# Two graph layers with residual normalisation: the rounding and splitting of x for group g+2 stands late in step g instead of at the begin of step g+1

## The chip, the cores and the metric

The kernel runs on one core of one Trainium2 chip. The metric is the device time in microseconds of one execution; lower is better.

## The reference

x has 128 graphs of 64 nodes with 512 features, in float32; adj is one 64 x 64 adjacency matrix with ones on its diagonal.

```python
x = layernorm(x + einsum('bnf,nm->bmf', x, adj * adj) + bias)        # layer 0, gives h
z_l, z_g, v = h @ W_lang.T, h @ W_grav.T, h @ W_V.T                  # layer 1
A_l = max(zn @ zn.T, 0) * not_eye             # zn: rows of z_l over their norms
A_g = exp(-|z_g[n] - z_g[m]|**2 / (2 sigma**2)) * not_eye
K = w_l * row_stochastic(A_l * adj) + (1 - w_l) * row_stochastic(A_g * adj)
out = layernorm(h + (K @ v) @ W_O.T)
```

## The kernel before

Two graphs fill the 128 partitions and make one pair p; four pairs make a group (NP = 4), and there are 16 groups (NG = 16). Every float32 matmul is made of three matmuls on rounded halves: each operand is split into a part _hi (rounded, by ScalarE) and a part _lo (the remainder, by VectorE, or by GpSimd for x), and hi·hi, hi·lo and lo·hi are added up in PSUM.

The weights are folded at the start, so that a group needs these pieces of work:

- x of a group comes in by one DMA into x_sb. ScalarE rounds it into x_hi (`split_x`, two instructions of 1024 columns), GpSimd subtracts into x_lo (`split_x`, four instructions of 512 columns).
- Layer 0: TensorE (`layer0`), VectorE adds the bias and takes statistics (`add_y`, `count_y`), GpSimd turns them into scales (`scale_y`), ScalarE normalises (`normalise_h`).
- h is transposed on TensorE (`transpose_h`) and split into hT_hi (ScalarE, `hi_hT`) and hT_lo (VectorE, `lo_hT`, L769).
- Twelve projections (`project` 0 to 11, L357) through a ring of three PSUM banks; each is split by `hi_proj` (ScalarE, L562) and `lo_proj` (VectorE, L774). Projection k may begin when `lo_proj` of the projection three before it is done.
- The Gram matrices of two pairs at a time (`gram` 0 and 1, L377) are copied out by ScalarE (`copy_p`); VectorE takes their diagonals (`diagonals`: four L784 instructions, then two L792) and GpSimd makes column factors of them (`columns`).
- Similarities, one group behind: TensorE transposes (`transpose_p`, L390 and L397), VectorE adds and weighs (`add_p` L805, `weigh` L812 and L816), forms sums and coefficients (`coefficients`, from L826 on) and K (`combine`, L843); TensorE transposes K (`transpose_k`, L408), it is split again (`hi_kt`, `lo_kt`), and `apply_k` (L421) multiplies.
- The result gets the residual, statistics, scales (`add_z`, `count_z`, `scale_z`) and `normalise_out`, and four DMAs store it.

A step g of the loop does the projections and Gram matrices of group g, layer 0 and the transposes of group g+1, and the similarities, K and the output of group g-1. The order on each engine is written out by hand and kept by semaphores alone; nothing reorders it. On TensorE a step runs: project 0, transpose_p(g-1, 0), project 1 to 3, transpose_p(g-1, 1), project 4, transpose_k(g-1, 0), project 5 and 6, apply_k 0 and 1, project 7, transpose_k(g-1, 1), layer 0 of pairs 0 and 1, project 8, apply_k 2 and 3, layer 0 of pairs 2 and 3, project 9 and 10, gram 0, transpose_h 0 and 1, project 11, transpose_h 2 and 3, gram 1. The last group has an order of its own, with no work for a group after it, and so no split of x; up to its project 6 the order on TensorE and up to transpose_k 0 that on VectorE is the one of a step.

Waits that matter here:

```python
# TensorE
project:     if k == 0: wait hT_split >= NP*g + NP        # all four lo_hT (L342)
             wait proj_split >= NPROJ*g + k - NRING + 1   # lo_proj three before (L347)
transpose_k: wait k_done; wait s2_done >= 2*g + 2         # add_p of both halves (L401, L404)
# VectorE
diagonals:   wait p_copied;   lo_hT: wait hT_hi_done;   lo_proj: wait proj_hi
# GpSimd
split_x:     wait x_hi_done >= 2*g + p//2 - 1
# the DMA queue of SyncE
load(g):     wait x_lo_done >= NP*g
```

Of the kernel before, what the change touches and what calls it, by code (L numbers as in the profile page):

```python
# [18 lines left out]
def bass_two_layer_graph_resnorm(  # L19
# [19 lines left out]
    NP = 4  # L39
    NG = B * N // (R * NP)  # L40
# [15 lines left out]
    def ring_of(k):  # L56

        return (NSETUP + k) % NRING
# [5 lines left out]
    with ctx:  # L64
# [182 lines left out]
        def out_rows(g):  # L247

            return x_sb if isinstance(g, int) and g == NG - 1 else o_sb
# [9 lines left out]
        def settle(engine):  # L259

            engine.nop(nofuse=True)
# [290 lines left out]
        def proj_dst(k, which):  # L552

            kind, j = PROJ[k]
            if kind == "u":
                return (u_hi, u_lo)[which][:, j, :]
            return (yT_hi, yT_lo)[which][:, j, kind, :]

        @block.scalar
        def _(act):  # L560
            def copy(dst, src, scale=1.0):
                return act.activation(dst, src, ACT.Copy, scale=scale)  # L562

            def split_x(g, c):
                if c == 0:
                    act.wait_ge(x_loaded, 16 * g)

                    act.wait_ge(l0_done, NP * g)
                s = slice(2 * c, 2 * c + 2)
                copy(x_hi[:, s, :], x_sb[:, s, :]).then_inc(x_hi_done, 1)  # L570
# [16 lines left out]
            def hi_proj(g, k):  # L587
                act.wait_ge(proj_done, NPROJ * g + k + 1)
                copy(proj_dst(k, 0), ring[ring_of(k)][:, :]).then_inc(proj_hi, 1)
# [8 lines left out]
            def exp_g(g, q):  # L598
                act.wait_ge(s2_done, 2 * g + q + 1)
                act.activation(E_g[:, :, :], S2[:, :, G, :], ACT.Exp, scale=inv_2s2[:, 0:1]).then_inc(exp_done, 1)  # L600

            def scale_l(g, q):
                act.wait_ge(coef_done, 2 * g + q + 1)
                for pp in range(2):
                    last = act.activation(K_l[:, pp, :], X_l[:, pp, :], ACT.Copy, scale=coef[:, pp:pp + 1])
                last.then_inc(kl_done, 1)
# [5 lines left out]
            def normalise_out(g, p):  # L612
                act.wait_ge(z_scale, 2 * g + p // 2 + 1)
                act.activation(out_rows(g)[:, p, :], out_rows(g)[:, p, :], ACT.Identity, scale=z_rs[:, p:p + 1],  # L614
                               bias=z_nb[:, p:p + 1]).then_inc(o_ready, 1)

            def step(g, par, tail=True):
                split_x(g + 1, 0)
                split_x(g + 1, 1)
                hi_proj(g, 0)  # L620
                hi_proj(g, 1)
                if tail:
                    exp_g(g - 1, 0)
                hi_proj(g, 2)
                if tail:
                    scale_l(g - 1, 0)
                hi_proj(g, 3)
                if tail:
                    exp_g(g - 1, 1)
                hi_proj(g, 4)  # L630
                if tail:
                    hi_kt(g - 1, 0)
                    scale_l(g - 1, 1)
                hi_proj(g, 5)
                hi_proj(g, 6)
                hi_proj(g, 7)
                if tail:
                    hi_kt(g - 1, 1)
                    normalise_out(g - 1, 0)
                    normalise_out(g - 1, 1)  # L640
                hi_proj(g, 8)
                normalise_h(g + 1, 1 - par, 0)
                normalise_h(g + 1, 1 - par, 1)
                if tail:
                    normalise_out(g - 1, 2)
                hi_proj(g, 9)
                if tail:
                    normalise_out(g - 1, 3)
                hi_proj(g, 10)
                copy_p(g, 0)  # L650
                normalise_h(g + 1, 1 - par, 2)
                normalise_h(g + 1, 1 - par, 3)
                hi_hT(g + 1, 1 - par, 0)
                hi_hT(g + 1, 1 - par, 1)
                hi_proj(g, 11)
                hi_hT(g + 1, 1 - par, 2)
                hi_hT(g + 1, 1 - par, 3)
                copy_p(g, 1)
# [43 lines left out]
                hi_hT(0, 0, p)  # L702
            hi_value(M_hi, 3 * DC)

            step(0, 0, tail=False)
            step(1, 1)
            with act.Fori(2, NG - 2, 2) as g:
                step(g, 0)
                step(g + 1, 1)
            step(NG - 2, 0)  # L710
            g = NG - 1
            hi_proj(g, 0)
            hi_proj(g, 1)
# [356 lines left out]
        @block.gpsimd  # L1070
        def _(pool):
            def split_x(g, p):
                pool.wait_ge(x_hi_done, 2 * g + p // 2 - 1)
                pool.tensor_tensor(x_lo[:, p, :], x_sb[:, p, :], x_hi[:, p, :], ALU.subtract).then_inc(x_lo_done, 1)  # L1074

            def scale_of(stats, ve_done, rs_done, scale, mv, ve, nm, rs, nb, d, q):

                pq = slice(2 * q, 2 * q + 2)
                pool.wait_ge(stats, d + 1)
                settle(pool)  # L1080
                pool.tensor_scalar(ve[:, pq], mv[:, pq, 1], LN_EPS, None, ALU.add).then_inc(ve_done, 1)  # L1081
                pool.wait_ge(ve_done, d + 1)
                pool.tensor_tensor(rs[:, pq], ve[:, pq], pow_neg_half[:, :], ALU.pow).then_inc(rs_done, 1)
                pool.tensor_scalar(nm[:, pq], mv[:, pq, 0], -1.0, None, ALU.mult).then_inc(rs_done, 1)
                pool.wait_ge(rs_done, 2 * d + 2)
                pool.tensor_tensor(nb[:, pq], nm[:, pq], rs[:, pq], ALU.mult).then_inc(scale, 1)  # L1086

            def scale_y(g, q):
                scale_of(y_stats, y_ve_done, y_rs_done, y_scale, y_mv, y_ve, y_nm, y_rs, y_nb, 2 * g + q, q)

            def scale_z(g, q):
                scale_of(z_stats, z_ve_done, z_rs_done, z_scale, z_mv, z_ve, z_nm, z_rs, z_nb, 2 * g + q, q)

            def columns(g, q):
                d = 2 * g + q
                pool.wait_ge(sq_done, d + 1)
                settle(pool)

                pool.tensor_scalar(sq_floor[q][:, :], sq[q][:, L, :], EPS * EPS, None, ALU.max).then_inc(floor_done, 1)
                pool.wait_ge(floor_done, d + 1)  # L1100
                pool.tensor_tensor(inv_norm[q][:, :], sq_floor[q][:, :], pow_neg_half[:, :],
                                   ALU.pow).then_inc(cols_ready, 1)

                pool.tensor_scalar(sq_eps[q][:, :], sq_floor[q][:, :], 2 * EPS, None, ALU.mult).then_inc(sq_eps_done, 1)
                pool.wait_ge(cols_ready, d + 1)
                pool.wait_ge(sq_eps_done, d + 1)
                pool.tensor_tensor(floors[q][:, 0:2], sq_eps[q][:, :], inv_norm[q][:, :],
                                   ALU.mult).then_inc(floors_ready, 1)

            def step(g, tail=True):  # L1110
                if tail:
                    columns(g - 1, 1)
                for p in range(NP):
                    split_x(g + 1, p)
                for q in range(2):
                    if tail:
                        scale_z(g - 1, q)
                    scale_y(g + 1, q)
                columns(g, 0)

            pool.memset(adj_bd[:, :], 0.0).then_inc(adj_zeroed, 1)
            pool.memset(ident[:, :], 0.0).then_inc(ident_ready, 1)
            pool.wait_ge(ident_ready, 1)
            pool.affine_select(out=ident[:, :], in_=ident[:, :], compare_op=ALU.not_equal, fill=1.0, base=0,
                               pattern=[[-1, R]], channel_multiplier=1).then_inc(ident_ready, 1)
            pool.memset(pow_neg_half[:, :], -0.5)
            pool.memset(floors[0][:, 2:4], EPS)
            pool.memset(floors[1][:, 2:4], EPS).then_inc(pow_ready, 1)
            pool.wait_ge(pow_ready, 1)
            for q in range(2):  # L1130
                scale_y(0, q)

            step(0, tail=False)
            step(1)
            with pool.Fori(2, NG - 2, 1) as g:
                step(g)
            step(NG - 2)
            g = NG - 1
            columns(g - 1, 1)
            scale_z(g - 1, 0)  # L1140
            columns(g, 0)
            columns(g, 1)
            scale_z(g - 1, 1)
            for q in range(2):

                pool.wait_ge(o_ready, NP * (g - 1) + 2 * q + 2)
                scale_z(g, q)
# [27 lines left out]
```

## Time and profile before

| | |
|---|---|
| device time, median of 3 runs | 702.46 us (702.32 to 703.02) |
| profiled execution | span 701.2 us from the first to the last instruction; no other time of it is given |
| TensorE busy | 671.6 us, 96% of the span |
| VectorE busy | 536.3 us, 76% |
| ScalarE busy | 345.4 us, 49% |
| GpSimd busy | 211.0 us, 30% |
| granted TensorE clock | 0.997 of full speed (mean) |
| one step in the middle, from project 0 to project 0 | 41.00 us |

Busy time is the time in which an engine had an instruction under way. Matmuls overlap, so that each has some 390 ns while the next one starts 230 ns after it. Of an instruction that is held up inside the engine, the time held up counts as its duration.

### The profile page before, as it was taken

Reading aid. Unit: us, or ns where it says so; the run is one execution under the profiler, and the core shown is the slowest. Engines: PE = TensorE matmul, PEld = TensorE weight load, DVE = VectorE, ACT = ScalarE, POOL = GpSimd, SP = SyncE. Lnnn points to the kernel's source line nnn. Section 1 sums busy time; section 2 is a strip of 40 time slices with the busy share of each in tenths; the row PEclk is TensorE's granted clock in tenths of the full one; section 3 lists DMA queues with packets and bytes.
Section 4 is the critical chain, followed back from the end, with each engine's and each line's share of the span. In section 5 each row is a group of like instructions: output and inputs, shape, how many; then the busy total and the mean of one; then the engine's idle time right before and its main releaser. Section 6 shows DMA issues by size and latency. Waiting matters only on the chain. (4 is left out here: it accounts for less than half of the span.)

```text
span 701.2 us, 11745 instructions
## 1 busy us (share of the span) xinstructions
PE 671.6 (96%) x3579; PEld 570.4 (81%) x3579; DVE 536.3 (76%) x1523; ACT 345.4 (49%) x614; POOL 211.0 (30%) x454
## 2 busy tenths in 40 slices
PE   8999999999999999999999999999999999999994
PEld 7888878787887878788787878878787887878883
DVE  6835795977879597786959778695977969697786
ACT  5633546355354535445453544545454454545433
POOL 0121413333341333334133333413333341233022
PEclk9999999999999999999999999999999999999998
DMA  7210020111102011110201111020111102001002
GB/s 286 91 38 24 5 86 31 61 60 61 61 3 87 30 60 60 60 60 0 90 30 60 60 60 60 0 90 30 60 60 60 55 5 90 31 0 61 0 31 91
DMA packets 20406, 38.33 MB, mean 55 GB/s; under 512 B 1824, under 2 KB 1824, under 8 KB 20384
## 3 DMA queue, kind: packets, MB, share of 16 engines
q1 hardware_dynamic: 20384, 38.05, 15.0%
q8 instruction: 12, 0.20, 0.1%
q14 instruction: 10, 0.08, 0.0%
HBM read 21.27 MB, written 16.78 MB: 54 GB/s over the span
## 5 line engine op out<-in xcount | busy, mean ns | idle before, releaser
L357 PE MATMUL ring<-hT_hi,T_hi 128*128 128x512 f32 x320 | 129.5, 405 | 0.0
L357 PE MATMUL ring<-hT_hi,T_lo 128*128 128x512 f32 x320 | 125.2, 391 | 0.0
L357 PE MATMUL ring<-hT_lo,T_hi 128*128 128x512 f32 x320 | 125.0, 391 | 0.0
L562 ACT ACTIVATE yT_hi<-ring 128x512 fp32r<-128x512 f32 x128 | 75.7, 591 | 71.0 <-PE ring L357 70.4
L774 DVE TENSOR_TENSOR yT_lo<-ring,yT_hi 128x512 fp32r<-128x512 f32 x128 | 86.1, 682 | 26.7 <-ACT yT_hi L562 26.7
L357 PE MATMUL ring<-M_hi,hT_hi 128*128 128x512 f32 x256 | 101.5, 397 | 0.0
L357 PE MATMUL ring<-M_hi,hT_lo 128*128 128x512 f32 x256 | 100.2, 391 | 0.0
L357 PE MATMUL ring<-M_lo,hT_hi 128*128 128x512 f32 x256 | 99.8, 390 | 0.0
L1074 POOL TENSOR_TENSOR x_lo<-x_sb,x_hi 128x512 fp32r<-128x512 f32 x60 | 77.0, 1315 | 18.5 <-ACT x_hi L562 18.5
L614 ACT ACTIVATE o_sb<-o_sb,z_nb,z_rs 128x512 f32<-128x512 f32 x60 | 47.1, 809 | 63.9 <-POOL z_nb L1086 63.9
L784 DVE CUSTOM_DVE_ANT_0 diag_scr<-P_sb,ident 128x128 f32<-128x128 f32 x128 | 29.7, 288 | 62.9 <-ACT P_sb L562 62.9
L1081 POOL TENSOR_SCALAR z_ve<-z_mv 128x2 f32<-128x2 f32 x32 | 7.0, 219 | 217.2 <-DVE z_mv L870 212.5
L377 PE MATMUL bank_p<-yT_hi,hT_hi 128*128 128x256 f32 x248 | 71.4, 288 | 0.1
L357 PEld LDWEIGHTS ring<-hT_hi,T_lo 128*128 128x128 f32 x320 | 60.1, 188 | 13.4
L357 PEld LDWEIGHTS ring<-hT_hi,T_hi 128*128 128x128 f32 x320 | 60.2, 188 | 12.7 <-DVE yT_lo L774 1.3
L377 PE MATMUL bank_p<-yT_hi,hT_lo 128*128 128x256 f32 x248 | 70.1, 283 | 0.0
L377 PE MATMUL bank_p<-yT_lo,hT_hi 128*128 128x256 f32 x248 | 70.1, 283 | 0.0
L357 PEld LDWEIGHTS ring<-hT_lo,T_hi 128*128 128x128 f32 x320 | 60.3, 188 | 10.6
L774 DVE TENSOR_TENSOR u_lo<-ring,u_hi 128x512 fp32r<-128x512 f32 x64 | 44.3, 692 | 26.7 <-ACT u_hi L562 26.5
L579 ACT ACTIVATE h_sb<-h_sb,y_nb,y_rs 128x512 f32<-128x512 f32 x64 | 48.7, 808 | 25.3 <-POOL y_nb L1086 25.3
L357 PEld LDWEIGHTS ring<-M_hi,hT_lo 128*128 128x128 f32 x256 | 48.0, 188 | 10.4
L357 PEld LDWEIGHTS ring<-M_lo,hT_hi 128*128 128x128 f32 x256 | 48.2, 188 | 9.9
(159 smaller groups left out, 1421.9 us busy)
## 6 DMA issues: line engine op xcount, KB each, us to landing
x_sb<-in_x_dram SPq DMA_DIRECT2D x15, 1024.0 KB, 5.2
out_dram<-o_sb SPq DMA_DIRECT2D x60, 256.0 KB, 2.0
x_sb<-in_x_dram SPq DMA_DIRECT2D x2, 512.0 KB, 5.2
w_raw<-in_L_gnn_W_lang_dram SPq DMA_DIRECT2D x1, 1024.0 KB, 6.2
o_sb<-in_L_gnn_W_grav_dram SPq DMA_DIRECT2D x1, 1024.0 KB, 8.6
h_sb<-in_L_gnn_W_V_dram SPq DMA_DIRECT2D x1, 1024.0 KB, 10.7
w_raw<-in_L_gnn_W_O_dram SPq DMA_DIRECT2D x1, 1024.0 KB, 7.8
out_dram<-x_sb SPq DMA_DIRECT2D x4, 256.0 KB, 2.0
```

The costliest lines, as they stand in the source:

```text
L357: last = pe.matmul(bank[:, :], a, b, start=n == 0, stop=n == len(terms) - 1)
L377: last = pe.matmul(p_bank(g, q)[:, pp, :, :], a, b, start=n == 0, stop=n == len(terms) - 1)
L562: return act.activation(dst, src, ACT.Copy, scale=scale)
L579: act.activation(h_sb[par][:, p, :], h_sb[par][:, p, :], ACT.Identity, scale=y_rs[:, p:p + 1], bias=y_nb[:, p:p + 1]).then_inc(h_ready, 1)
L614: act.activation(out_rows(g)[:, p, :], out_rows(g)[:, p, :], ACT.Identity, scale=z_rs[:, p:p + 1], bias=z_nb[:, p:p + 1]).then_inc(o_ready, 1)
L774: dve.tensor_tensor(proj_dst(k, 1), ring[ring_of(k)][:, :], proj_dst(k, 0), ALU.subtract).then_inc(proj_split, 1)
L784: last = dve.tensor_tensor_reduce(out=diag_scr[:, 2 * pp + s, :], in0=P_sb[q][:, pp, s, :], in1=ident[:, :], scale=1.0, scalar=0.0, op0=AL ...
L1074: pool.tensor_tensor(x_lo[:, p, :], x_sb[:, p, :], x_hi[:, p, :], ALU.subtract).then_inc(x_lo_done, 1)
L1081: pool.tensor_scalar(ve[:, pq], mv[:, pq, 1], LN_EPS, None, ALU.add).then_inc(ve_done, 1)
```

## The change

`split_x` of ScalarE for the next group stood at the head of a step, ahead of `hi_proj(g, 0)`. Now step g holds the one for group g+2, behind `normalise_out(g-1, 3)` and ahead of `hi_proj(g, 10)`. On GpSimd the four instructions stood behind `columns(g-1, 1)`; now they stand behind `scale_y(g+1, 1)` and ahead of `columns(g, 0)`. Group 1 is split ahead of step 0, and step 14 splits nothing. The waits in `split_x` are the same: x has landed, layer 0 of the group before is done (it frees x_hi and x_lo), and for GpSimd x_hi is there. The load of the next x waits for x_lo as before.

```diff
@@ ScalarE
-            def step(g, par, tail=True):
-                split_x(g + 1, 0)
-                split_x(g + 1, 1)
+            def step(g, par, tail=True, ahead=True):
                 hi_proj(g, 0)
                 hi_proj(g, 1)
...
                 hi_proj(g, 9)
                 if tail:
                     normalise_out(g - 1, 3)
+                if ahead:
+                    split_x(g + 2, 0)
+                    split_x(g + 2, 1)
                 hi_proj(g, 10)
                 copy_p(g, 0)
...
+            split_x(1, 0)
+            split_x(1, 1)
             step(0, 0, tail=False)
...
-            step(NG - 2, 0)
+            step(NG - 2, 0, ahead=False)
@@ GpSimd
-            def step(g, tail=True):
+            def step(g, tail=True, ahead=True):
                 if tail:
                     columns(g - 1, 1)
-                for p in range(NP):
-                    split_x(g + 1, p)
                 for q in range(2):
                     if tail:
                         scale_z(g - 1, q)
                     scale_y(g + 1, q)
+                if ahead:
+                    for p in range(NP):
+                        split_x(g + 2, p)
                 columns(g, 0)
...
+            for p in range(NP):
+                split_x(1, p)
             step(0, tail=False)
...
-            step(NG - 2)
+            step(NG - 2, ahead=False)
```

## Rows read from the trace of the kernel before

**Rows 1.** The page: busy time, share of the span and instructions of each engine
```profile
PE 671.6 (96%) x3579; PEld 570.4 (81%) x3579; DVE 536.3 (76%) x1523; ACT 345.4 (49%) x614; POOL 211.0 (30%) x454
```

**Rows 2.** Waits of TensorE: what waited for what, us in total, times, longest
```profile
PE bank_pt L408 <- DVE S L805: 17.1, 14, 1.2
```

**Rows 3.** Timeline of TensorE in two steps: start us, us, instruction, [idle before <-releaser]
```profile
290.13 0.38 PE L397 MATMUL bank_r<-ident,inv_norm 128*128 128x128 f32 x2
290.48 0.50 PE L357 MATMUL ring<-hT_hi,T_hi 128*128 128x512 f32 x1
...
331.25 0.38 PE L397 MATMUL bank_r<-ident,inv_norm 128*128 128x128 f32 x2
331.47 0.50 PE L357 MATMUL ring<-hT_hi,T_hi 128*128 128x512 f32 x1
...
334.10 0.39 PE L357 MATMUL ring<-hT_hi,T_lo 128*128 128x512 f32 x1
335.73 0.41 PE L408 MATMUL bank_pt<-ident,K_sb 128*128 128x128 f32 x2 [1.24 <-DVE S L805]
```

**Rows 4.** Timeline of VectorE in that step, up to that wait
```profile
328.72 0.78 DVE L816 CUSTOM_DVE_ANT_0 X_l<-X,mask 128x128 f32<-128x128 f32 x1
...
329.44 1.37 DVE L816 CUSTOM_DVE_ANT_0 X_l<-X,mask 128x128 f32<-128x128 f32 x1
...
330.74 0.68 DVE L774 TENSOR_TENSOR yT_lo<-ring,yT_hi 128x512 fp32r<-128x512 f32 x1
331.34 0.76 DVE L826 SCALAR_TENSOR_TENSOR X_g<-E_g,mask 128x128 f32<-128x128 f32 x1
...
334.90 0.68 DVE L805 TENSOR_TENSOR S<-bank_pt,P_sb 128x512 f32<-128x512 f32 x1
```

**Rows 5.** Timeline of GpSimd around that step's begin
```profile
313.74 0.20 POOL L1086 TENSOR_TENSOR y_nb<-y_nm,y_rs 128x2 f32<-128x2 f32 x1
...
326.81 5.14 POOL L1074 TENSOR_TENSOR x_lo<-x_sb,x_hi 128x512 fp32r<-128x512 f32 x4
```

**Rows 6.** Timeline of VectorE in the last group, the same stretch
```profile
657.13 0.29 DVE L816 CUSTOM_DVE_ANT_0 X_l<-X,mask 128x128 f32<-128x128 f32 x1
...
661.25 0.68 DVE L805 TENSOR_TENSOR S<-bank_pt,P_sb 128x512 f32<-128x512 f32 x1
```

**Rows 7.** Timeline of TensorE in the last group, the same stretch
```profile
659.66 0.38 PE L397 MATMUL bank_r<-ident,inv_norm 128*128 128x128 f32 x2
659.79 0.47 PE L357 MATMUL ring<-hT_hi,T_hi 128*128 128x512 f32 x1
...
662.40 0.39 PE L357 MATMUL ring<-hT_hi,T_lo 128*128 128x512 f32 x1
662.63 0.38 PE L408 MATMUL bank_pt<-ident,K_sb 128*128 128x128 f32 x2
```

**Rows 8.** Timeline of ScalarE, late in a step and at the next begin
```profile
312.36 0.81 ACT L614 ACTIVATE o_sb<-o_sb,z_nb,z_rs 128x512 f32<-128x512 f32 x1
...
316.19 0.60 ACT L562 ACTIVATE P_sb<-bank_p 128x512 f32<-128x512 f32 x1 [2.35 <-PE bank_p L377]
...
323.98 2.00 ACT L562 ACTIVATE x_hi<-x_sb 128x1024 fp32r<-128x1024 f32 x2
```

**Rows 9.** Timeline of VectorE, late in the step: diagonals to lo_hT
```profile
316.82 0.29 DVE L784 CUSTOM_DVE_ANT_0 diag_scr<-P_sb,ident 128x128 f32<-128x128 f32 x1 [2.26 <-ACT P_sb L562]
...
317.86 0.48 DVE L792 TENSOR_SCALAR P_sb<-P_sb,sq 128x128 f32<-128x128 f32 x2
318.71 0.69 DVE L769 TENSOR_TENSOR hT_lo<-bank_x,hT_hi 128x512 fp32r<-128x512 f32 x1 [0.37 <-ACT hT_hi L562]
...
321.57 0.68 DVE L769 TENSOR_TENSOR hT_lo<-bank_r,hT_hi 128x512 fp32r<-128x512 f32 x1
```

**Rows 10.** Timeline of TensorE, the begin of the next step's project 0
```profile
323.28 0.40 PE L357 MATMUL ring<-hT_hi,T_hi 128*128 128x512 f32 x1
```

**Rows 11.** GpSimd's subtractions, all: xcount, ns min/median/max, first and last start us
```profile
L1074 POOL TENSOR_TENSOR x_lo<-x_sb,x_hi x60: 1280/1301/1354, 43.9 to 618.0; 128x512 fp32r<-128x512 f32 x60
```

## The prediction, made before the result was known

> **What bounds the kernel now.** I began with the page. TensorE is busy for 671.6 of 701.2 us and no other engine passes 76% [rows 1], so a change pays only where TensorE stands still, or costs where it makes it stand still. The next view is TensorE's waits. One line carries nearly all of it: transpose_k (L408) waits for VectorE's add_p (L805), 14 times, 17.1 us in all, never over 1.2 us [rows 2]. Fourteen times is once in each of steps 1 to 14. The timeline of one step shows its true size: the matmul before it starts at 334.10, transpose_k at 335.73 [rows 3], 1.63 us apart, where the same two stand 0.23 us apart when nothing is late [rows 7]. So the stall is 1.40 us (the view of waits counts from the modelled end of the matmul, some 0.16 us later: 17.1 / 14 = 1.22, and 1.22 + 0.16 = 1.38). Over 14 steps I take 14 x 1.38 = 19.3 us.
>
> A second, small one stands just ahead: project 4 after transpose_p(g-1, 1) starts 0.22 us after L397 in one step and 0.35 us in its neighbour [rows 3], where 0.13 us is undisturbed [rows 7]. Project 4 waits for lo_proj 1, which is the L774 from 330.74 to 331.42 [rows 4], 0.05 us before 331.47. That is 0.09 and 0.22 us in turn, 7 x 0.31 = 2.2 us; call it 2.0, since step 14 has the small value.
>
> Why is VectorE late? Its timeline has two L816 of 0.78 and 1.37 us and one L826 of 0.76 us [rows 4]. In the last group the same L816 takes 0.29 us [rows 6]. GpSimd tells the rest: its four subtractions for x_lo run from 326.81 to 331.95, without a gap, 1.3 us each [rows 5, 11], so they end near 328.1, 329.4, 330.7 and 331.95. The slow instructions end at 329.50, 330.81 and 332.10: each some 0.15 us behind the end of one GpSimd instruction. VectorE is held until the GpSimd instruction under way is over, and gets in one such instruction between two of GpSimd's. The L774 in the middle, which has one input in PSUM, keeps its 0.68 us [rows 4]. L816 and L826 have both inputs in SBUF. Lost: (0.78 - 0.29) + (1.37 - 0.29) + (0.76 - 0.29) = 2.04 us in each step.
>
> The last group is the experiment that the kernel makes by itself: it has no x_lo beside it. There add_p ends at 661.93 [rows 6], 0.70 us before transpose_k wants to start, and both stalls are gone [rows 7].
>
> **What the change removes.** The x_lo work leaves the stretch of L816 and L826. VectorE gets its 2.04 us back, more than the 1.40 us that TensorE waits, and the last group shows the margin that is left, 0.70 us. Both stalls vanish in the 14 steps: 19.3 + 2.0 = 21.3 us. The two ScalarE roundings, 2.00 us from 323.98 [rows 8], also leave the step's begin. That is worth nothing: they lay in ScalarE's idle time before project 0 was done, and VectorE's lo_proj 0 then waits for TensorE anyhow, in the last group too, where they are missing.
>
> **What it adds: the new place.** On ScalarE normalise_out(g-1, 3) ends at 313.17 [rows 8]. Two roundings follow, 313.1 to 315.1, then hi_proj 10 of some 0.6 us (the length of the copy at 316.19) to 315.7. copy_p waits for gram 0 until 316.19 [rows 8], so it isn't moved, and nothing behind it is. Their cover is the 2.35 us for which ScalarE idled ahead of that copy; without it, they would push hi_hT and the lo_hT behind it.
>
> GpSimd is free from 313.94 [rows 5]. It starts when the first rounding of 1.0 us is done, at about 314.19, and needs 5.14 us as before [rows 5]: pieces end near 315.5, 316.8, 318.05 and 319.33. Beside them VectorE does `diagonals`: four L784 from 316.82 [rows 9]. L784 is the same custom operation as L816, with both inputs (P_sb, ident) in SBUF, so I let it be held the same way. In the trace before no L784 has an x_lo beside it. Bounds: each at 0.29 us as now (no hold), or held to the end of the last GpSimd piece. I take the second, by the row of L816. The third piece is under way at 316.82: the first L784 ends at 318.2, the second at 319.33 + 0.15 = 319.48, the others 0.21 us apart at 319.69 and 319.91, instead of 317.75 (0.11 us ahead of L792 at 317.86 [rows 9]). So VectorE is 2.16 us late there.
>
> By the Trainium skill ("SBUF — State Buffer", Who interferes with whom) a VectorE instruction with two SBUF inputs contends with a GpSimd instruction that reads SBUF, and the second to issue blocks fully. By that rule L784 collides in its new company as L816 did in the old; it gives the same sum as the row of L816, and speaks against getting the full 21.3 us. No row of L784 shows it yet.
>
> What is behind L784 on VectorE: two L792, then lo_hT 0 and 1, lo_proj 11, lo_hT 2 and 3. The L792 start 0.11 us after the last L784, and the next could follow 0.40 us later. The five run at 0.60 us intervals, and the last takes 0.68. So the last lo_hT ends 0.51 + 4 x 0.60 + 0.68 = 3.59 us after the last L784: 323.50. Today it ends at 322.25, since it holds two pauses of 0.37 us for ScalarE (the one before 318.71 is in [rows 9], the other stands before lo_proj 11). Project 0 of the next step waits for it and starts at 323.28 now [rows 10]. With some 0.1 us from VectorE's end to TensorE's start (0.15 between L805 and L408 [rows 3, 4]) it starts at 323.60: a new stall of 0.3 us. In steps 1 to 14 that is 14 x 0.3 = 4.2 us.
>
> Who else waits: `columns(g, 0)` on GpSimd moves behind x_lo and the late diagonals, from 317.9 to about 320.0. Its four small instructions take under 2 us, and its reader, transpose_p, stands behind project 0, which begins at 323.3 and lasts 2.8 us. SyncE's load for the next x is released by x_lo near 319.4 instead of 331.95, after the four stores of that step, and its data is wanted some 35 us later. It costs nothing, and a transfer of 5 us could be late by 30 before it did. Ahead of step 0 the split of group 1 is what step 0 did first, at the same place.
>
> **The sum.** Span 701.2 - 21.3 + 4.2 = 684.1 us. The span misses 1.26 us of the median (702.46); I keep this: 685.4 us.
>
> **The rivals.**
>
> *A. As above*, both stalls gone, a new one of 0.1 to 0.7 us before project 0: 682.6 to 691.0, likeliest 685.4.
>
> *B. The new place is free*: L784 isn't held, or fewer pieces hit it. VectorE has 1.03 us between 322.25 and 323.28, and 0.74 us of pauses; a delay under 1.7 us doesn't show. Then 702.46 - 21.3 = 681.2 us. For it: my value of 2.16 us is only 0.4 us past this. Against it: 316.82 falls right behind the begin of the third piece.
>
> *C. The stall moves and eats the gain*, one mechanism: x_lo starts later than 314.2, since the roundings stand behind two normalise_out, which hang on a chain of statistics through VectorE and GpSimd. Each us later is one us more of stall, as the diagonals can't end before the last piece. At x_lo from 315.4 on the new stall is 1.5 us and the change is worth nothing: 702.5 us. In between, at 0.8 to 1.4 us, 692.4 to 700.8.
>
> *D. Slower*: VectorE holds GpSimd up as well. If three of the four pieces each waited for one VectorE instruction of 0.7 us, x_lo would end 2.1 us later, the new stall would be 2.4 us, and the time 702.46 - 21.3 + 14 x 2.4 = 714.8 us. It decides from 1.2 us of such delay on. Against it: 60 pieces lie between 1280 and 1354 ns, with VectorE busy beside most of them [rows 11].
>
> *E. VectorE's gain is not what frees transpose_k*: then only the new stall counts, 702.46 + 4.2 = 706.7. The last group speaks against it.
>
> **How the numbers follow.** A 0.66, B 0.19, C's gains 0.07 and its point of no gain 0.02, D 0.04, E 0.02. The predicted time is that of A. For the range I take B whole (681.2, less 0.5 for phase) and A up to its bound of a 0.7 us stall: 680.7 to 691.0; what is left out, C, D and E, is 0.15. Of no change I call what lies within 0.2%, 1.4 us, about what a measurement of this kernel can tell. Faster: A, B and C's gains, 0.92. Same 0.03. Slower 0.05.
>
> **What the profile after would show.** Right: L816 at 0.29 us everywhere and no wait of L408 on L805; L784 with maxima near 1.3 us in `diagonals(g, 0)`, and the L784 of `diagonals(g, 1)` at 0.29; a new wait of TensorE at project 0 (L357) on hT_lo (L769), some 0.3 us, 14 times; a step of about 39.8 us instead of 41.0; x_lo starting 9.1 us before the last gram's end. Wrong: L784 at 0.29 throughout (B), x_lo starting less than 8.2 us before the last gram's end, or pieces of x_lo over 1.6 us (C, D), or L408 still waiting (E).

## The result and the profile after

| | median | runs | |
|---|---|---|---|
| before | 702.54 us | 4 | 702.32 to 703.02 |
| changed | 685.2 us | 4 | 684.88 to 685.32 |

The ratio is 0.975, with a 95% interval of 0.9739 to 0.9761: 17.3 us faster, where 17.1 were forecast (702.46 - 685.4). The profiled execution took 685.29 us with a span of 683.5 us. In the changed kernel the lines of VectorE and GpSimd stand three or more further down: `diagonals` is L787 (was L784), `weigh` L819 (L816), `coefficients` L829 (L826), `lo_hT` L772 (L769), x_lo L1077 (L1074).

TensorE's share on the page, to be read beside [rows 1]:

```profile
PE 669.0 (98%) x3579; PEld 571.0 (84%) x3579; DVE 532.2 (78%) x1523; ACT 345.6 (51%) x614; POOL 210.4 (31%) x454
```

The waits of TensorE. The row of transpose_k in [rows 2] is gone, and in the loop one wait long enough for this view is left, at project 0 (L357). The other rows belong to the setup ahead of the loop, or, at L421, to the last group:

```profile
PE ring L475 <- DVE yT_lo L947: 1.9, 1, 1.9
PE bank_r L483 <- POOL ident L1128: 1.7, 1, 1.7
PE bank_r L421 <- issue: 0.8, 1, 0.8
PE ring L357 <- DVE hT_lo L772: 0.5, 1, 0.5
...
```

The timeline of TensorE at the two places of [rows 3], now back to 0.14 and 0.23 us:

```profile
324.32 0.38 PE L397 MATMUL bank_r<-ident,inv_norm 128*128 128x128 f32 x2
324.46 0.47 PE L357 MATMUL ring<-hT_hi,T_hi 128*128 128x512 f32 x1
...
327.06 0.39 PE L357 MATMUL ring<-hT_hi,T_lo 128*128 128x512 f32 x1
327.29 0.38 PE L408 MATMUL bank_pt<-ident,K_sb 128*128 128x128 f32 x2
```

The durations of `weigh` and `diagonals` over the whole run (count, then ns min/median/max). `weigh` (L819) has lost its long ones, `diagonals` (L787) has them now:

```profile
L819 DVE CUSTOM_DVE_ANT_0 X_l<-X,mask x64: 284/291/295, 82.7 to 665.1; 128x128 f32<-128x128 f32 x64
...
L787 DVE CUSTOM_DVE_ANT_0 diag_scr<-P_sb,ident x128: 280/289/1375, 70.8 to 660.2; 128x128 f32<-128x128 f32 x128
```

The late place itself, first GpSimd, then VectorE beside it, to be read against [rows 9]:

```profile
306.86 5.10 POOL L1077 TENSOR_TENSOR x_lo<-x_sb,x_hi 128x512 fp32r<-128x512 f32 x4 [0.25 <-ACT x_hi L562]
312.70 0.30 POOL L1102 TENSOR_SCALAR sq_floor<-sq 128x2 f32<-128x2 f32 x1 [0.74 <-DVE sq L787]
```

```profile
309.61 1.20 DVE L787 CUSTOM_DVE_ANT_0 diag_scr<-P_sb,ident 128x128 f32<-128x128 f32 x1 [0.68 <-ACT P_sb L562]
...
310.74 1.37 DVE L787 CUSTOM_DVE_ANT_0 diag_scr<-P_sb,ident 128x128 f32<-128x128 f32 x1
...
312.04 0.28 DVE L787 CUSTOM_DVE_ANT_0 diag_scr<-P_sb,ident 128x128 f32<-128x128 f32 x1
...
312.25 0.28 DVE L787 CUSTOM_DVE_ANT_0 diag_scr<-P_sb,ident 128x128 f32<-128x128 f32 x1
...
313.05 0.68 DVE L772 TENSOR_TENSOR hT_lo<-bank_x,hT_hi 128x512 fp32r<-128x512 f32 x1
...
315.44 0.68 DVE L772 TENSOR_TENSOR hT_lo<-bank_r,hT_hi 128x512 fp32r<-128x512 f32 x1
```

The last of four GpSimd pieces ends at 311.96. Two of the four L787 are held, 1.20 and 1.37 us, and the second ends at 312.11, 0.15 us behind the piece. The diagonals take 2.92 us instead of 0.93. The last lo_hT ends at 316.12, and TensorE's project 0 starts 0.13 us later, at 316.25:

```profile
315.96 0.28 PE L377 MATMUL bank_p<-yT_hi,hT_lo 128*128 128x256 f32 x1
316.25 0.49 PE L357 MATMUL ring<-hT_hi,T_hi 128*128 128x512 f32 x1
316.58 0.40 PE L357 MATMUL ring<-hT_lo,T_hi 128*128 128x512 f32 x1
```

0.29 us lie between 315.96 and 316.25, where matmuls of the gram stand 0.12 us apart: a stall of 0.17 us. A stall read in this way, from the distance of two starts, is called a stall by the starts below. The modelled end of the last gram matmul (0.28 us) swallows it, so the view of waits doesn't list it; it is found by the starts alone.

### The profile page after: what moved, and what is told of

Same layout as the page of the kernel before. It is cut to its first block, busy times and chain, and to the rows that moved or that the text cites. A ratio compares the mean times of both kernels' runs of the same rounds, so it can differ in the third digit from the quotient of the medians.

```text
span 683.5 us, 11745 instructions
## 1 busy us (share of the span) xinstructions
PE 669.0 (98%) x3579; PEld 571.0 (84%) x3579; DVE 532.2 (78%) x1523; ACT 345.6 (51%) x614; POOL 210.4 (31%) x454
## 4 chain that ended last, share of the span: by engine, by line
PE 92%; DVE 3%; ACT 2%; DMA 1%; issue 1%; POOL 1%; SPq 0%; POOLq 0%; DVEq 0%
PE ring L357 56%; PE bank_p L377 12%; PE ring L475 4%; PE bank_x L318 3%; PE bank_p L318 3%; PE bank_k L421 3%; PE bank_r L421 3%; PE bank_pt L390 2%; PE bank_r L397 1%; DMA w_raw<-in_L_gnn_W_lang_dram 1%; PE bank_pt L336 1%; PE bank_r L336 1%; PE bank_k L336 1%; PE bank_pt L408 1%; PE bank_x L336 1%
## 5 line engine op out<-in xcount | busy, mean ns | idle before, releaser
L357 PE MATMUL ring<-hT_hi,T_hi 128*128 128x512 f32 x320 | 130.5, 408 | 0.6 <-DVE hT_lo L772 0.5
L357 PE MATMUL ring<-hT_hi,T_lo 128*128 128x512 f32 x320 | 125.4, 392 | 0.0
L357 PE MATMUL ring<-hT_lo,T_hi 128*128 128x512 f32 x320 | 124.7, 390 | 0.0
L777 DVE TENSOR_TENSOR yT_lo<-ring,yT_hi 128x512 fp32r<-128x512 f32 x128 | 87.5, 684 | 35.3 <-ACT yT_hi L562 35.3
L357 PE MATMUL ring<-M_hi,hT_hi 128*128 128x512 f32 x256 | 101.5, 396 | 0.0
L357 PE MATMUL ring<-M_hi,hT_lo 128*128 128x512 f32 x256 | 100.2, 391 | 0.0
L357 PE MATMUL ring<-M_lo,hT_hi 128*128 128x512 f32 x256 | 99.9, 390 | 0.0
L1077 POOL TENSOR_TENSOR x_lo<-x_sb,x_hi 128x512 fp32r<-128x512 f32 x60 | 76.4, 1301 | 22.4 <-ACT x_hi L562 22.4
L787 DVE CUSTOM_DVE_ANT_0 diag_scr<-P_sb,ident 128x128 f32<-128x128 f32 x128 | 56.4, 495 | 28.0 <-ACT P_sb L562 28.0
L357 PEld LDWEIGHTS ring<-hT_hi,T_hi 128*128 128x128 f32 x320 | 60.1, 188 | 13.6 <-issue 3.0
L357 PEld LDWEIGHTS ring<-hT_hi,T_lo 128*128 128x128 f32 x320 | 60.1, 188 | 13.4
L357 PEld LDWEIGHTS ring<-hT_lo,T_hi 128*128 128x128 f32 x320 | 60.3, 188 | 10.8
L357 PEld LDWEIGHTS ring<-M_hi,hT_lo 128*128 128x128 f32 x256 | 48.0, 188 | 10.3
L357 PEld LDWEIGHTS ring<-M_lo,hT_hi 128*128 128x128 f32 x256 | 48.1, 188 | 9.9
```

Of the source, the lines that this page charges most:

```text
L357: last = pe.matmul(bank[:, :], a, b, start=n == 0, stop=n == len(terms) - 1)
L777: dve.tensor_tensor(proj_dst(k, 1), ring[ring_of(k)][:, :], proj_dst(k, 0), ALU.subtract).then_inc(proj_split, 1)
L787: last = dve.tensor_tensor_reduce(out=diag_scr[:, 2 * pp + s, :], in0=P_sb[q][:, pp, s, :], in1=ident[:, :], scale=1.0, scalar=0.0, op0=AL ...
```

## The experiments

The time agrees with the forecast, but an agreement of one sum proves none of its terms. The theory is that GpSimd's subtractions hold VectorE's instructions with two inputs in SBUF, at the old place and at the new. Its rivals: ScalarE's roundings ahead of hi_proj 0 were the cost; any work of GpSimd would hold VectorE; or the small remainder at project 0 has another cause. The first four kernels ran on one chip (before: 702.64 us there), the last four on one chip as well (before: 702.76 us). Code cuts leave lines out at "...", and the declarations of a scratch tile and of semaphores.

### The roundings alone moved

```diff
 # on the kernel before; GpSimd unchanged
@@ ScalarE, step(g)
-                split_x(g + 1, 0)
-                split_x(g + 1, 1)
                 hi_proj(g, 0)
...
                     normalise_out(g - 1, 3)
+                if ahead:
+                    split_x(g + 2, 0)
+                    split_x(g + 2, 1)
                 hi_proj(g, 10)
```

> The kernel before, with ScalarE's roundings of x (x_hi of g+2) in the new late place and GpSimd's four subtractions left at the begin of the step. Theory (the subtractions hold VectorE's L816 and L826): nothing is gained, 701.5 to 703.5 us, L816 keeps its 0.8 and 1.4 us and transpose_k still waits 1.4 us in 14 steps. Rival (ScalarE's 2.0 us ahead of hi_proj 0 were what made the step late): most of the gain comes from this alone, 684 to 690 us.

Measured: 702.73 us, ratio 0.9999 (0.9989 to 1.0008). No part of the gain comes from moving ScalarE's roundings alone. The wait of transpose_k is as before, and `weigh` is still held:

```profile
PE bank_pt L408 <- DVE S L808: 17.3, 14, 1.3
```

```profile
L819 DVE CUSTOM_DVE_ANT_0 X_l<-X,mask x64: 283/293/1373, 82.1 to 682.4; 128x128 f32<-128x128 f32 x64
```

It also shows that the roundings cost nothing at the late place.

### The subtractions made tiny, at the old place

```diff
 # on the kernel before
-    pool.tensor_tensor(x_lo[:, p, :], x_sb[:, p, :], x_hi[:, p, :], ALU.subtract)
+    pool.tensor_tensor(x_lo[:, p, 0:2], x_sb[:, p, 0:2], x_hi[:, p, 0:2], ALU.subtract)
```

> The kernel before, with GpSimd's four subtractions of the loop on 2 of 512 columns each (the rest of x_lo keeps what group 0 left there), everything at its old place, ScalarE's roundings at the begin of the step too. Theory: both waits of TensorE go, 702.5 - 21.3 = 681.2 us. Rival (ScalarE's roundings at the begin cost something as well): over 684 us, with a wait left in the first projections.

Measured: 680.7 us (680.6 to 680.87), ratio 0.9683 (0.9666 to 0.9699). This is the price of the subtractions at the old place: 702.64 - 680.7 = 21.9 us, against 21.3 forecast. No wait of transpose_k is left, with ScalarE's roundings at the step's begin, and no L816 is held:

```profile
L816 DVE CUSTOM_DVE_ANT_0 X_l<-X,mask x64: 284/291/295, 82.2 to 660.6; 128x128 f32<-128x128 f32 x64
```

### GpSimd busy, but only writing

```diff
 # on the kernel before, in split_x of GpSimd; x_lo becomes zero
-    pool.tensor_tensor(x_lo[:, p, :], x_sb[:, p, :], x_hi[:, p, :], ALU.subtract).then_inc(x_lo_done, 1)
+    settle(pool)
+    pool.memset(scratch[:, :], 0.0).then_inc(scratch_done, 1)      # 1024 columns
+    pool.wait_ge(scratch_done, NP * (g - 1) + p + 1)
+    settle(pool)
+    pool.memset(x_lo[:, p, :].bitcast(fp32), 0.0).then_inc(x_lo_done, 1)
```

> The kernel before, with each subtraction replaced by two GpSimd memsets (1024 columns of a scratch tile, then the 512 of x_lo, which is thus zero), so GpSimd is busy at the old place and writes SBUF but reads nothing there. Theory that VectorE's second SBUF input shares a read path with GpSimd: L816 and L826 at 0.29 us although memsets run beside them, no wait of transpose_k, 681 to 683 us. Rival (any GpSimd instruction beside holds VectorE, or memory traffic as such): L816 ends each time just behind the end of a memset, and transpose_k waits again, in so far as the memsets reach to 328.7 and beyond in the step.

Measured: 680.69 us, ratio 0.9683 (0.9662 to 0.9703), the time of the kernel with tiny subtractions. GpSimd was busy over the same stretch, some 1.5 us for each pair. Its timeline in one step, and VectorE's beside it:

```profile
160.63 0.96 POOL L1077 MEMSET scratch<- 128x1024 f32 x1
161.70 0.53 POOL L1080 MEMSET x_lo<- 128x512 f32 x1
162.17 0.95 POOL L1077 MEMSET scratch<- 128x1024 f32 x1
```

```profile
161.01 0.29 DVE L818 CUSTOM_DVE_ANT_0 X_l<-X,mask 128x128 f32<-128x128 f32 x1
...
162.04 0.28 DVE L828 SCALAR_TENSOR_TENSOR X_g<-E_g,mask 128x128 f32<-128x128 f32 x1
...
162.25 0.29 DVE L828 SCALAR_TENSOR_TENSOR X_g<-E_g,mask 128x128 f32<-128x128 f32 x1
```

L818 lies wholly inside the memset from 160.63 to 161.59 and takes its 0.29 us; the L828 at 162.25 lies inside the one from 162.17. Over the whole run none of them is held, and transpose_k doesn't wait:

```profile
L818 DVE CUSTOM_DVE_ANT_0 X_l<-X,mask x64: 283/290/294, 82.0 to 660.4; 128x128 f32<-128x128 f32 x64
...
L828 DVE SCALAR_TENSOR_TENSOR X_g<-E_g,mask x64: 280/286/291, 83.1 to 661.9; 128x128 f32<-128x128 f32 x64
```

So it is not GpSimd's activity as such, nor its writing, that holds VectorE. What differs is that a memset reads nothing from SBUF. It is also another operation in pieces of other lengths; no run here tells the reading from these. The result fits the sentence of the Trainium skill ("SBUF — State Buffer", Who interferes with whom) that a VectorE instruction with two SBUF inputs contends with a GpSimd instruction that reads SBUF and not with one that only writes it; here 1.37 us beside the subtraction and 0.29 beside the memset.

### One piece more at the late place

```diff
 # on the changed kernel, GpSimd, ahead of the four subtractions
+                    pool.wait_ge(x_hi_done, 2 * g + 3)
+                    pool.tensor_tensor(x_lo[:, 0, :], x_sb[:, 0, :], x_hi[:, 0, :], ALU.subtract).then_inc(extra_done, 1)
+                    pool.wait_ge(extra_done, g + 1)
                     for p in range(NP):
                         split_x(g + 2, p)
```

> The changed kernel with one more subtraction of 512 columns (the one of pair 0 done twice) ahead of the four in the late place, so that the last piece ends 1.3 to 1.4 us later. Theory (project 0 waits for lo_hT, which waits for the diagonals, which wait for the last piece): the wait of 0.2 us becomes 1.5 to 1.6, and the time 685.2 + 14 x 1.35 = 704 us, the whole gain gone. Rival (there is slack behind the diagonals, and the 0.2 us at project 0 has another cause): under 690 us.

Measured: 701.4 us (701.22 to 701.72), ratio 0.998 (0.997 to 0.9989). One more subtraction of 1.3 us on an engine that is 31% busy costs 16 us, nearly the whole gain. TensorE's wait is where the theory puts it:

```profile
PE ring L358 <- DVE hT_lo L773: 17.1, 13, 1.4
```

It is in 13 steps, not 14, which is half of the difference to the 704 us expected. The other half: against the 685.29 us of the changed kernel measured again (below), each costs 16.1 / 13 = 1.24 us on average instead of 1.35. In step 0 there is no output of a group before, so ScalarE and GpSimd get to the split earlier: the first subtraction starts 11.1 us ahead of project 0 of step 1.

### The changed kernel again, and its subtractions made tiny

> The changed kernel once more, on the chip of the three below: 685.2 us, ratio 0.975, project 0 late by 0.17 us in most steps.

Measured: 685.29 us (684.96 to 685.41), ratio 0.9752 (0.9738 to 0.9765). Its trace has the same 13 stalls at project 0, eleven of them of 0.15 to 0.19 us.

```diff
 # on the changed kernel
-    pool.tensor_tensor(x_lo[:, p, :], x_sb[:, p, :], x_hi[:, p, :], ALU.subtract)
+    pool.tensor_tensor(x_lo[:, p, 0:2], x_sb[:, p, 0:2], x_hi[:, p, 0:2], ALU.subtract)
```

> The changed kernel with the four subtractions of the loop on 2 of 512 columns each (the rest of x_lo keeps what group 0 left there). It prices all that x_lo still costs in the late place. Theory: the wait at project 0 (2.7 us in sum over the steps in the trace) goes, 682.5 us. Rival (the late place costs more than that wait, for example through ScalarE's late hi_proj 10): no gain over 685.2, or a wait left elsewhere.

Measured: 680.77 us (680.6 to 680.94). It is the same time as with tiny subtractions at the old place (680.7), so ScalarE's roundings and the earlier load of x cost nothing in either place. The subtractions cost 685.29 - 680.77 = 4.5 us at the new place. I had expected 2.7, the sum of the stalls by the starts. What I left out is that TensorE starts up less densely after a wait: the first matmul at 316.25 is followed after 0.33 us, and without the wait, in this kernel, after 0.24:

```profile
313.76 0.40 PE L357 MATMUL ring<-hT_hi,T_hi 128*128 128x512 f32 x1
314.00 0.40 PE L357 MATMUL ring<-hT_lo,T_hi 128*128 128x512 f32 x1
```

A stall of 0.17 us thus costs 0.27: steps of 39.75 us against 39.48. Twelve such steps and one of 0.7 (below) make some 3.9 us. The traces agree: from project 0 of step 1 to that of step 15 it is 556.7 us in the changed kernel, 556.9 in its second run, and 552.8 with tiny subtractions, 3.9 and 4.1 more. The other 0.4 to 0.6 us of the medians lie outside this stretch and aren't settled. They can be scatter of the setup: project 0 of step 1 starts at 77.31 and 76.79 us in the two traces of the same changed kernel, and between 76.6 and 77.3 in those of all these kernels.

### Two pieces ahead of columns, two behind

```diff
 # on the changed kernel, GpSimd, step(g)
                 if ahead:
-                    for p in range(NP):
+                    for p in range(2):
                         split_x(g + 2, p)
                 columns(g, 0)
+                if ahead:
+                    for p in range(2, NP):
+                        split_x(g + 2, p)
```

> The changed kernel with the subtractions of pairs 0 and 1 ahead of columns(g, 0) on GpSimd and those of pairs 2 and 3 behind it. Theory: pieces 0 and 1 end some 0.2 us before the diagonals begin, and pieces 2 and 3 lie beside lo_hT and lo_proj 11, which have an input in PSUM and aren't held; L787 (the diagonals) at 0.29 us, no wait at project 0, 682.5 us, faster than both kernels. Rival (lo_hT is held as well, or columns(g, 0) ends so late that diagonals(g, 1) is hit): 685 us or more.

Measured: 681.1 us (680.58 to 681.35), ratio 0.9689 (0.9676 to 0.9702). Faster than both kernels, with the whole computation done. GpSimd in one step, then VectorE:

```profile
304.85 2.54 POOL L1077 TENSOR_TENSOR x_lo<-x_sb,x_hi 128x512 fp32r<-128x512 f32 x2 [0.26 <-ACT x_hi L562]
...
310.42 2.54 POOL L1077 TENSOR_TENSOR x_lo<-x_sb,x_hi 128x512 fp32r<-128x512 f32 x2
```

```profile
307.62 0.29 DVE L787 CUSTOM_DVE_ANT_0 diag_scr<-P_sb,ident 128x128 f32<-128x128 f32 x1 [0.69 <-ACT P_sb L562]
...
310.12 0.68 DVE L772 TENSOR_TENSOR hT_lo<-bank_k,hT_hi 128x512 fp32r<-128x512 f32 x1
311.17 0.69 DVE L777 TENSOR_TENSOR u_lo<-ring,u_hi 128x512 fp32r<-128x512 f32 x1 [0.37 <-ACT u_hi L562]
311.78 0.68 DVE L772 TENSOR_TENSOR hT_lo<-bank_pt,hT_hi 128x512 fp32r<-128x512 f32 x1
...
317.68 0.69 DVE L777 TENSOR_TENSOR yT_lo<-ring,yT_hi 128x512 fp32r<-128x512 f32 x1 [1.23 <-ACT yT_hi L562]
```

The first two pieces end at 307.39, 0.23 us ahead of the diagonals. Over the whole run one L787 is held, 0.70 us in step 1. The other two pieces run from 310.42 to 312.96 beside lo_hT and lo_proj 11, which have one input in PSUM and keep their 0.68 us.

### All four behind columns

```diff
 # on the changed kernel, GpSimd, step(g)
-                if ahead:
-                    for p in range(NP):
-                        split_x(g + 2, p)
                 columns(g, 0)
+                if ahead:
+                    for p in range(NP):
+                        split_x(g + 2, p)
```

> The changed kernel with all four subtractions behind columns(g, 0). They start some 0.3 us behind the time at which columns(g, 0) ended in the kernel before, 3.6 us ahead of project 0, and end 1.6 us behind its begin, where diagonals(g, 1) has begun 0.8 us earlier on VectorE. Theory: diagonals(g, 0) is free, so no wait at project 0; the first L787 of diagonals(g, 1) is held some 0.8 us, which VectorE's 1.2 us pause ahead of lo_proj 0 takes up: 682.5 to 683.5 us. Rival: the late diagonals(g, 1) delay columns(g, 1) and transpose_p, or the whole chain to transpose_k: over 686 us.

Measured: 680.84 us (680.52 to 680.99), ratio 0.9687 (0.9673 to 0.97). The last piece ends at 315.16 and holds the first L787 of diagonals(g, 1):

```profile
314.62 0.70 DVE L787 CUSTOM_DVE_ANT_0 diag_scr<-P_sb,ident 128x128 f32<-128x128 f32 x1 [1.86 <-ACT P_sb L562]
...
317.37 0.69 DVE L777 TENSOR_TENSOR yT_lo<-ring,yT_hi 128x512 fp32r<-128x512 f32 x1 [0.82 <-ACT yT_hi L562]
```

0.41 us are lost there, and VectorE's pause ahead of lo_proj 0, which was 1.23 us in the two-and-two kernel, is 0.82: the loss disappears in it. A hold by itself costs nothing; it costs where no pause long enough stands between it and TensorE. Both orders reach the time of the kernels with tiny subtractions within 0.4 us, so no more than that is left to be had from where x_lo stands.

## Why the prediction was right, point by point

**Both stalls go, 21.3 us.** Right: 21.9 us measured (702.64 - 680.7). The missing 0.6 us are 0.04 us a step. That is about the size of TensorE's slower start after a wait, for which I had no term: in the trace before, the next instruction behind each of the two stalled places stands 0.02 to 0.03 us further off than with tiny subtractions, together some 0.7 us in 14 steps. The two stalls themselves, by the starts, add up to the 19.3 and 2.0 us of the prediction.

**VectorE's 2.04 us of held L816 and L826 are the cause, and the margin after is enough.** Right. Making the subtractions tiny removes the wait; replacing them by work that only writes removes it too; moving ScalarE's part does not. That the hold comes from reading SBUF is the explanation that fits best, not more.

**ScalarE's roundings are worth nothing at either place.** Right: ratio 0.9999.

**x_lo starts 9.1 us ahead of the end of the last gram.** Right: 306.86 against 316.08 (315.96 + 0.12), 9.22 us.

**L784 is held like L816, 2.16 us late.** Right in kind and nearly in size: the first two held, 1.20 and 1.37 us, the diagonals 1.99 us late. From the last of them to the end of the last lo_hT it takes 312.53 to 316.12, the 3.59 us of the prediction.

**A new stall of 0.3 us in 14 steps, 4.2 us.** The sum is near (4.5 us measured), but partly by luck, since its parts were off in both ways. The stall is 0.17 us in most steps, with 0.10 on top for the start after it. It is in 13 steps, not 14. That it is 0.17 and not 0.3 us comes for the most part from x_lo, which starts 0.13 us earlier than forecast against the gram's end. By the starts the 13 stalls add up to 2.6 us, not 4.2; the slower start after them gives 1.3 more. And behind step 1 the stall is 0.7 us. The timeline of GpSimd and of TensorE there, in the changed kernel:

```profile
108.29 5.13 POOL L1077 TENSOR_TENSOR x_lo<-x_sb,x_hi 128x512 fp32r<-128x512 f32 x4 [0.69 <-ACT x_hi L562]
```

```profile
116.69 0.28 PE L377 MATMUL bank_p<-yT_hi,hT_lo 128*128 128x256 f32 x1
117.51 0.49 PE L357 MATMUL ring<-hT_hi,T_hi 128*128 128x512 f32 x1 [0.54 <-DVE hT_lo L772]
```

x_lo starts 8.5 us ahead of the gram's end (116.81) instead of 9.2; the diagonals begin while its second piece is under way, and three of them are held. GpSimd's last scale of the output (z_nb) starts 27.7 us behind project 0 there, and 27.1 us in a step of the middle; why isn't settled. That step behaves in kind as rival C said, with x_lo late behind normalise_out: 0.7 us later, and 0.5 us more of stall. The kernel with one piece more shows the slope for all steps.

**The other costs at nothing** (columns, the load of x, now issued at 312.12, right behind the last piece, and hi_proj 10): right in sum. Tiny subtractions give the same time at both places, which covers the load and hi_proj 10. They don't delay `columns`; for it speaks only that the 0.27 us a step are all found at project 0, as 0.17 of stall and 0.10 of start. None was tried by itself.

**Rivals.** B (681.2 us, the new place is free) didn't come true in the changed kernel, but it is the time that the two other orders reach (681.1 and 680.84). Its bound, a delay under 1.7 us that doesn't show, was a little low by the prediction's own rows: 2.16 us gave 0.3 of stall there, so the room was some 1.85. Measured: 1.99 late, 0.17 of stall, 1.82 of room. D didn't occur: in the changed kernel too the pieces take at most 1354 ns, beside held and unheld instructions. E is refuted by the tiny subtractions. The chances of D and E add up to 0.06, where the prediction gives 0.05 to slower.

**The agreement within 0.2 us.** That is luck: the gain was put 0.6 us too low and the cost 0.3 too low, and the two miss in opposite directions. The mechanism was right in both places. The step that was missing is TensorE's slower start after a wait; the one that was mis-sized is the new stall.

## What to carry to other kernels

When an instruction of VectorE with two inputs in SBUF takes several times its usual time in part of its places, look what GpSimd does at the moment it ends: if it ends just behind GpSimd instructions that read SBUF, as here, the instruction is probably held, and the order of the two can be worth more than their busy shares say. Put such GpSimd work beside VectorE instructions that have an input in PSUM, or ahead of a pause of VectorE, and price a place by the pause that follows it, not by the time that is lost in it. For a bound, make the suspected work tiny at its place: here one such run at each place told that 21.9 us were to be had and that the change left 4.5 of them.

## What the runs showed of the hardware

A GpSimd memset beside VectorE's two-input instructions cost these nothing (0.29 us), a GpSimd subtraction up to 1.37 us, although both kept GpSimd busy at the same place. The held instruction ends 0.15 us behind the end of the GpSimd instruction under way, and one gets through between two of them.

TensorE loses up to 0.1 us more here than the time it waits: behind a stall of 0.17 us the second matmul starts 0.33 us after the first, in place of 0.24. And a stall of the size of the modelled overlap of two matmuls (0.28 us long and 0.12 us apart in the gram, so 0.16 us) doesn't appear among the waits; 12 of 13 stalls here, of 0.08 to 0.18 us, were visible by their starts alone.
